# Graph counting stage: tile steps spread over twelve pairs, projection evicted by ScalarE

## The chip, the cores and the metric

The kernel runs on one core of one Trainium2 chip. The metric is the device time of the whole program in microseconds (us). A core has five engines that run side by side and meet only at semaphores: TensorE (PE in the profile, PEld its weight loads) multiplies into eight PSUM banks, VectorE (DVE) and ScalarE (ACT) do elementwise work, GpSimd (POOL) and SyncE (SP) mostly move data here.

## The reference, cut to what matters

Two graph layers, each followed by a mixture-of-experts layer, on 1250 nodes with 512 features and 40000 edges. What the change touches is the first layer:

```python
for h in range(8):                                   # heads
    Wx = x @ Ws[h] + Wb[h]                           # x: layer-normed rows, [1250, 64] per head
    s = Wx[v_tgt] @ a_w[h, :d] + Wx[v_src] @ a_w[h, d:] + a_b[h]
    alpha = segment_softmax(leaky_relu(s), v_tgt)    # over the edges of a target
    outs.append(segment_sum(alpha * Wx[v_src], v_tgt))
```

The kernel never gathers by edge. It first counts how many edges run from each source to each target, a dense matrix of counts, and does the softmax and the sums with matmuls on that matrix.

## The kernel before, in words

The nodes are ten tiles of 128. The **counting stage** works off 184 *pairs* (a group of 384 sorted edges with a window of 16 targets), in 23 batches of eight. For a pair VectorE writes one-hot matrices of the edges' sources and targets (`onehot`), TensorE multiplies them, three matmuls of 160 columns (`count`), and adds what the window already holds with an identity matmul (`merge`), and ScalarE writes the sum back (`write_batch`). A batch's one-hots are written in two halves of four pairs. A half waits for `counted` at a pair about two batches back, since the one-hots have two buffers; `merge(k)` waits until ScalarE has written pair k-2. Each batch TensorE and ScalarE load eight window addresses into registers at its sixth pair (`targets`).

Everything else of the first layer's front half is threaded between the pairs. For a tile t: VectorE takes the row statistics (`ln_stats`), ScalarE a square root (`ln_sqrt`), VectorE the reciprocal (`ln_scale`), ScalarE writes the normed rows (`ln_norm`), TensorE transposes them into bank 6 (`tile_T`), ScalarE copies the upper fp16 part (`ln_copy`), VectorE makes the lower part (`xT_low`), and TensorE then does twelve products of 512 columns with the projection weights, each with one of 16 columns for the attention scores (`lin_a`, j from 0 to 11). Last, the two sums are scaled and get their bias (`evac_a`, on VectorE). In the kernel before one tile is begun per batch: `BEGIN` puts tile t at batch 1+t, its transposes at the third pair of batch 2+t, its products in batch 3+t by `LIN_SLOTS`, its eviction into the middle of batch 5+t. So ten batches carry tiles, and the last ones hold only the second layer's weight transposes (`second_weights`, four steps, from batch 12), the score thresholds, and the exponentials with two loads of ScalarE's function table (batches 19 and 20).

Each engine runs its own list in the order written. After the last pair is written (`hist_done`) all engines turn to the per-head matmuls.

Of the kernel before, what the change touches and what calls it, by code (L numbers as in the profile page):

```python
# [8 lines left out]
F16 = mybir.dt.float16  # L9
# [5 lines left out]
P = 128  # L15
# [15 lines left out]
LB = 8  # L31
# [24 lines left out]

BEGIN = {1 + t: t for t in range(T)}
LIN_SLOTS = ((0,), (1, 2), (), (3, 4), (5, 6), (7,), (8, 9), (10, 11))
B_GW = max(BEGIN) + 2
B_CS = B_GW + K  # L60
B_EXP = B_CS + 3
AHEAD = 3
# [4 lines left out]
def gnn_ffn_kernel(nc, x_d, src_d, dst_d, Ws_d, Wb_d, aw_d, ab_d, Wg_d, bg_d, We_d, be_d, gW_d, gb_d,  # L67
                   Wr_d, br_d, W1_d, b1_d, W2_d, b2_d, out_d):
    ctx = ExitStack()
    with ctx:  # L70
# [92 lines left out]
        hi16, o = carve(num_words, o, [GE], F16)  # L163
        src_i = be_bc[:, 0:GE].bitcast(I32)
        VP, o = carve(big, 0, [T, 2, H, 2, FE], F16)
        nacc, o = carve(big, o, [T, H, FE])
# [249 lines left out]
        def _(g):  # L416
# [15 lines left out]
            nc.gpsimd.iota(iota_lo, [[1, P]], base=0, **kw)  # L432
            nc.gpsimd.memset(ones16, 1.0)
            nc.gpsimd.iota(iota_q, [[1, RW]], base=1, **kw).then_inc(sem("consts"), 1)
            nc.gpsimd.memset(zero[:, 0, :], 0.0).then_inc(sem("zero_set"), 1)
# [77 lines left out]
        def _(a):  # L513
# [26 lines left out]
            def exponential(i):  # L540
# [7 lines left out]
                if i == 3:  # L548
                    act(A2, e2t, ACT.Exp).then_inc(sem("exps"), 1)

            def write_batch(base, at, middle):

                for k in range(LB):
                    if not isinstance(base, int):
                        a.wait_ge(sem("counted"), base + (k + 1))
                    ins = act(counts_at(at[k], k), count_bank(base, k)[:, 0:RW].rearrange("p (d s) -> p s d", s=T), ACT.Copy)  # L556
                    if isinstance(base, int):
                        ins.wait_op(sem("counted"), base + (k + 1), "sem-ge")
                    ins.then_inc(sem("written"), 1)
                    middle(k)  # L560
# [37 lines left out]
            for b in range(NB):  # L598
                if b in BEGIN:
                    ln_sqrt(BEGIN[b])  # L600

                def middle(k):
                    if k == 1 and b - 1 in BEGIN:
                        t = BEGIN[b - 1]
# [7 lines left out]
                    if k == 3 and b - 1 in BEGIN:  # L612
                        t = BEGIN[b - 1]
# [8 lines left out]
                if b == 1:  # L622
                    a.wait_ge(sem("wa_psum"), 1)
                    act(Wa[:, 0, :, :].rearrange("p k c -> p (k c)"), bank[5][:, 0:K * 2 * H], ACT.Copy, scale=WS)
                    act(cb, bank[5][:, K * 2 * H:(K + 1) * 2 * H], ACT.Copy).then_inc(sem("weight_hi"), 1)
                if b - B_GW in range(K):
# [207 lines left out]
        def _(v):  # L834
# [146 lines left out]
            def value(h):  # L981

                if h:
                    v.wait_ge(sem("v_lo"), h)
                V.tensor_tensor(vtmp, Wx[:, :, h, :].unsqueeze(1).to_broadcast([P, 2, T, FE]),  # L985
                                bc(B12[:, :, :, h], [P, 2, T, FE]), ALU.mult).then_inc(sem("v_made"), 1)

            pair_tables(0)
            for b in range(NB):
                if b == 1:  # L990
                    v.wait_ge(sem("ld_x"), 64)
                if b in BEGIN:
                    ln_stats(BEGIN[b], x[:, BEGIN[b], :])
                if b - 2 - B_GW in range(K):
# [4 lines left out]
                if b == NB - 1:  # L999
                    last_onehots(b)  # L1000
                elif b:
                    half_onehots(b, 0)
                    if b - 4 in BEGIN:
                        evac_a(BEGIN[b - 4])
                        if BEGIN[b - 4] == T - 1:
                            scores()
                    half_onehots(b, 1)
# [9 lines left out]
                if b == 3:  # L1017
                    v.wait_ge(sem("weight_hi"), 2)
                    V.scalar_tensor_tensor(Wa[:, 1, :, :].rearrange("p k c -> p (k c)"), bank[5][:, 0:K * 2 * H], WS,
                                           Wa[:, 0, :, :].rearrange("p k c -> p (k c)"), ALU.mult, ALU.subtract).then_inc(sem("weight_lo"), 1)  # L1020
                if b - 1 in BEGIN:
                    ln_scale(BEGIN[b - 1])
                if b - 2 in BEGIN:
                    t = BEGIN[b - 2]
                    xT_low(t, bank[6], xTs[:, t % 2, :, :, :])
            v.wait_ge(sem("exps"), 4)
# [330 lines left out]
        def _(pe):  # L1357
# [39 lines left out]
            def lin_a(t, j):  # L1397
                k, i = divmod(j, len(PASSES))
                xp, wp = PASSES[i]
                if j == 0:  # L1400
                    if t == 0:
                        pe.wait_ge(sem("weight_lo"), 2)
                    pe.wait_ge(sem("xT_ready"), t + 1)
                    if t >= 2:
                        pe.wait_ge(sem("evacA"), t - 1)
                xt = xTs[:, t % 2, xp, k, :]
                last = j == K * len(PASSES) - 1
                mm(bank[2 + t % 2][:, :], xt, W016[:, wp, k, :], start=j == 0, stop=last)  # L1408
                ins = mm(bank[4 + t % 2][:, 0:2 * H], xt, Wa[:, wp, k, :], start=j == 0, stop=last)
                if last:  # L1410
# [15 lines left out]
            def thresholds():  # L1426
                pe.wait_ge(sem("thr_made"), 1)
                pe.wait_ge(sem("weight_lo"), 2 + K)
                for i, n in enumerate((4, 4, 2)):
# [52 lines left out]
            def between(b, k):  # L1482
                if b - 2 in BEGIN:
                    for j in LIN_SLOTS[k]:
                        lin_a(BEGIN[b - 2], j)
                if k == 2 and b - 1 in BEGIN:
                    t = BEGIN[b - 1]
# [344 lines left out]
```

## Time and profile before

| | us |
|---|---|
| median of 3 runs | 567.69 (564.15, 567.69, 568.19) |
| the profiled execution's own time | 565.49 |
| its span in the trace | 563.7 |
| counting stage: first count to the write of the last pair | 21.4 to 146.8 |
| busy: TensorE, VectorE, ScalarE over the span | 88%, 84%, 61% |

In the rows of a timeline the first number is the start in us from the span's start, the second how long the row's instructions took together; "[0.43 <-PE ...]" is idle time before it and what ended it. Instructions of one engine overlap a little, so what one adds to its engine is read from start to start. TensorE's busy time shows matmuls in flight, and is no measure of how much more fits in.

### The profile page before, as it was taken

Reading aid. Unit: us, or ns where it says so; the run is one execution under the profiler, and the core shown is the slowest. Engines: PE = TensorE matmul, PEld = TensorE weight load, DVE = VectorE, ACT = ScalarE, POOL = GpSimd, SP = SyncE. Lnnn points to the kernel's source line nnn. Section 1 sums busy time; section 2 is a strip of 40 time slices with the busy share of each in tenths; the row PEclk is TensorE's granted clock in tenths of the full one; section 3 lists DMA queues with packets and bytes.
Section 4 is the critical chain, followed back from the end, with each engine's and each line's share of the span. In section 5 each row is a group of like instructions: output and inputs, shape, how many; then the busy total and the mean of one; then the engine's idle time right before and its main releaser. Section 6 shows DMA issues by size and latency. Waiting matters only on the chain.

```text
span 563.7 us, 12125 instructions
## 1 busy us (share of the span) xinstructions
PE 498.4 (88%) x4635; PEld 369.9 (66%) x4636; DVE 473.0 (84%) x933; ACT 342.4 (61%) x663; POOL 68.7 (12%) x83
## 2 busy tenths in 40 slices
PE   1869999877589999999889899988899999889995
PEld 1757777666488888889767644444466696557662
DVE  7999999799899999995899758995877787768771
ACT  5365555567889999995575533344545457756820
POOL 3000000000000000000000020223244420212242
PEclk9999999999899999999999989999999999999998
DMA  6980000002001111100000068000001119776111
GB/s 175 351 290 2 1 2 1 2 6 93 3 27 66 53 48 49 49 3 1 1 1 2 0 215 325 1 1 1 4 20 59 57 55 354 262 234 222 60 53 52
DMA packets 25306, 45.14 MB, mean 80 GB/s; under 512 B 6961, under 2 KB 7205, under 8 KB 25248
## 3 DMA queue, kind: packets, MB, share of 16 engines
q1 hardware_dynamic: 23264, 39.16, 20.4%
q0 software_dynamic: 1952, 5.18, 2.5%
q8 instruction: 39, 0.64, 0.5%
q14 instruction: 19, 0.16, 0.1%
q10 hardware_dynamic: 32, 0.01, 0.0%
HBM read 33.23 MB, written 11.95 MB: 80 GB/s over the span
## 4 chain that ended last, share of the span: by engine, by line
PE 52%; DVE 33%; issue 8%; ACT 3%; DMA 2%; POOL 1%; ACTq 0%; SPq 0%; POOLq 0%; DVEq 0%
PE bank L1384 7%; PE bank L1774 7%; PE bank L1650 5%; PE bank L1408 5%; PE bank L1451 4%; DVE work L1080 4%; DVE big L948 4%; PE bank L1745 4%; PE bank L1458 4%; PE bank L1555 3%; PE bank L1362 3%; PE bank L1568 2%; DVE rings L1080 2%; DVE st L847 2%; DVE work L985 1%
## 5 line engine op out<-in xcount | busy, mean ns | idle before, releaser
L948 DVE TENSOR_TENSOR big<-mid 128x1536 f16<-128x1536 f16 (+1 forms) x100 | 92.0, 979 | 0.0
L1555 PE MATMUL bank<-big,work 128*128 128x130 f16 x1080 | 67.3, 224 | 8.4 <-DVE work L1080 8.4
L1451 PE MATMUL bank<-big 128*128 128x160 f16 x552 | 70.9, 245 | 4.1 <-DVE big L948 4.1
L1555 PEld LDWEIGHTS bank<-big,work 128*128 128x128 f16 x1080 | 64.1, 100 | 10.4 <-DVE work L1080 4.9
L1451 PEld LDWEIGHTS bank<-big 128*128 128x128 f16 x552 | 50.9, 110 | 6.7 <-DVE big L948 6.3
L657 ACT ACTIVATE mid<-aux,small 128x1280 f16<-128x1280 f32 x36 | 47.4, 1349 | 0.7 <-DVE work L1080 0.4
L1568 PE MATMUL bank<-big,mid 128*128 128x260 f16 x400 | 47.1, 275 | 0.1
L1650 PE MATMUL bank<-mid 128*128 128x512 f16 x200 | 47.2, 378 | 0.0
L556 ACT ACTIVATE big<-bank 128x160 f32 x92 | 27.9, 303 | 26.7 <-PE bank L1458 25.3
L556 ACT ACTIVATE mid<-bank 128x160 f32 x92 | 27.7, 302 | 25.5 <-PE bank L1458 22.5
L1568 PEld LDWEIGHTS bank<-big,mid 128*128 128x128 f16 x400 | 38.2, 96 | 7.5 <-issue 0.3
L518 ACT ACTIVATE sd<-ve 128x1 f32<-128x1 f32 x40 | 8.0, 200 | 51.6 <-DVE ve L849 51.6
L1408 PE MATMUL bank<-big,rings 128*128 128x512 f16 x120 | 38.6, 378 | 0.0
L1458 PE MATMUL bank<-mid,ident 128*128 x92 | 27.7, 302 | 9.1 <-ACT mid L556 4.8
L847 DVE BATCH_NORM_STATS2 st<-row 128x6 f32<-128x512 f32 x40 | 27.6, 691 | 8.5 <-POOL row L489 7.8
L1555 PE MATMUL bank<-big,rings 128*128 128x130 f16 x520 | 32.0, 220 | 2.6 <-DVE rings L1080 1.6
L531 ACT ACTIVATE rings<-row,nm,rs 128x512 f32<-128x512 f32 x30 | 24.3, 810 | 13.5 <-DVE nm L865 13.5
L1555 PEld LDWEIGHTS bank<-big,rings 128*128 128x128 f16 x520 | 29.9, 98 | 3.7 <-DVE rings L1080 2.2
L1650 PEld LDWEIGHTS bank<-mid 128*128 128x128 f16 x200 | 19.7, 104 | 18.0
L473 POOL DMA_INDIRECT out<-aux x16 | 22.2, 1388 | 76.6 <-DVE aux L1303 74.2
L457 POOL TENSOR_TENSOR mid<-mid,ident 128x128 f16<-128x128 f16 x10 | 3.9, 424 | 215.9 <-DVE small L1134 215.9
L523 ACT ACTIVATE rings<-bank 128x512 f16<-128x512 f32 (+1 forms) x30 | 17.8, 593 | 18.3 <-PE bank L1362 18.3
(313 smaller groups left out, 1122.9 us busy)
## 6 DMA issues: line engine op xcount, KB each, us to landing
big<-in_L_ffn_W SPq DMA_DIRECT2D x10, 1024.0 KB, 8.8
mid<-in_L_ffn_W SPq DMA_DIRECT2D x6, 1024.0 KB, 14.4
xperm_scratch<-work SPq DMA_DIRECT2D x1, 5753.0 KB, 19.4
aux<-thr_scratch SPq DMA_DIRECT2D x8, 640.0 KB, 3.8
aux<-xperm_scratch SPq DMA_DIRECT2D x8, 523.0 KB, 3.8
row<-in_x SPq DMA_DIRECT2D x1, 2304.0 KB
aux<-in_L_gnn_Ws SPq DMA_DIRECT2D x4, 256.0 KB, 4.5
work<-in_L_gnn_W SPq DMA_DIRECT2D x1, 1024.0 KB, 14.6
```

The costliest lines, as they stand in the source:

```text
L556: ins = act(counts_at(at[k], k), count_bank(base, k)[:, 0:RW].rearrange("p (d s) -> p s d", s=T), ACT.Copy)
L657: act(zmask[i % NZ], thr_bc[:, h % 2, :], ACT.Sigmoid, bias=steep[:, s, h:h + 1], scale=-STEEP).then_inc(sem("z_made"), 1)
L847: link(V.bn_stats(st[:, i, :], xt))
L948: return V.tensor_tensor(out.rearrange("p c (v two) -> p c v two", two=2), values.rearrange("p (v two) -> p v two", two=2).unsqueeze(1).to ...
L1384: ins = mm(out, xt16[:, xp, k, :], w16[:, wp, k, :], start=i == 0 and k == 0, stop=i == 2 and k == K - 1)
L1408: mm(bank[2 + t % 2][:, :], xt, W016[:, wp, k, :], start=j == 0, stop=last)
L1451: mm(count_bank(base, k)[:, 0:RW], L_ring[:, slot, k * CH + j, :], R_ring[:, slot, k * CH + j, :], start=j == 0, stop=False)
L1458: ins = mm(count_bank(base, k)[:, 0:RW].rearrange("p (d s) -> p s d", s=T), ident16[:, :], counts_at(at[k], k), start=False, stop=True)
L1555: ins = mm(acc_region(h, t), weighted[i % NC][:, t * P:(t + 1) * P], VP[:, s, part, h, :, :].rearrange("p b f -> p (b f)"), start=False, s ...
L1568: ins = mm(bank[2 * (t % 2) + g2][:, 0:4 * FE].rearrange("p (h f) -> p h f", f=FE), C[:, s, t * P:(t + 1) * P], VP[:, s, part, 4 * g2:4 * ...
L1650: ins = mm(bank[6 + t % 2][:, :], C[:, s, t * P:(t + 1) * P], hp[:, s, part, :], start=s == 0 and part == 0, stop=s == T - 1 and part == 1)
L1774: ins = mm(bank[4 + 2 * (e % 2) + j][0:m, :], hT16[:, e % 2, hp_, k, j * P:j * P + m], W16[e % 2][1][:, wp, k, :], start=False, stop=n == ...
```

## The change

The schedule of a tile is no longer bound to batches. Tables give each step its place: VectorE's by half batches (`STATS_H`, `SCALE_H`, `LOW_H`, every three halves), ScalarE's and TensorE's by pairs (`SQRT_P`, `NORM_P`, `ROWS_P`, `COPY_P`, `LIN_P`, `EVAC_P`, every twelve pairs). The ten tiles so take pairs 24 to 143 instead of 24 to 103. The eviction is ScalarE's, a plain scaled copy; the bias is added by TensorE as one more product ahead of the twelve (its two fp16 parts stand in 64 partitions of `Wb16` and `cb16`). VectorE makes the lower parts of these once, at batch 2. The second layer's weight steps begin at batch 17 instead of 12, `scores` moves to batch 19, the exponentials to batch 21, the second table load to batch 22.

```diff
-BEGIN = {1 + t: t for t in range(T)}
-LIN_SLOTS = ((0,), (1, 2), (), (3, 4), (5, 6), (7,), (8, 9), (10, 11))
-B_GW = max(BEGIN) + 2
+HALF = LB // 2
+STEP = 3 * HALF
+STATS_H = {2 + 3 * t: t for t in range(T)}
...
+LOW_H = {6 + 3 * t: t for t in range(T)}
+SQRT_P = {7 + STEP * t: t for t in range(T)}
+NORM_P = {15 + STEP * t: t for t in range(T)}
+ROWS_P = {17 + STEP * t: t for t in range(T)}
+COPY_P = {18 + STEP * t: t for t in range(T)}
+LIN_SLOTS = ((0,), (1,), (2,), (3,), (4,), (), (5,), (6,), (7,), (8, 9), (10,), (11,))
+LIN_P = {24 + STEP * t + i: (t, js) for t in range(T) for i, js in enumerate(LIN_SLOTS)}
+EVAC_P = {24 + STEP * (t + 1): t for t in range(T)}
+SCORES_H = max(EVAC_P) // HALF + 2
+B_GW = max(ROWS_P) // LB + 2
...
+            def evac_a(t):
+
+                a.wait_ge(sem("linA"), t + 1)
+                act(Wx[:, t, :, 0:F], bank[2 + t % 2][:, :].rearrange("p (h f) -> p h f", h=H), ACT.Copy, scale=1.0 / WS)
+                act(sc[:, t, :], bank[4 + t % 2][:, 0:2 * H], ACT.Copy, scale=1.0 / WS).then_inc(sem("evacA"), 1)
...
-                act(cb, bank[5][:, K * 2 * H:(K + 1) * 2 * H], ACT.Copy).then_inc(sem("weight_hi"), 1)
+                act(cb16[0:64, :], bank[5][0:64, K * 2 * H:(K + 1) * 2 * H], ACT.Copy, scale=WS)
+                a.wait_ge(sem("ld_x"), 64)
+                act(Wb16[0:64, :], Wb_bc[0:64, :, :].rearrange("p h f -> p (h f)"), ACT.Copy, scale=WS).then_inc(sem("weight_hi"), 1)
...
-            def evac_a(t):
-                v.wait_ge(sem("linA"), t + 1)
-                V.scalar_tensor_tensor(Wx[:, t, :, 0:F], bank[2 + t % 2][:, :].rearrange("p (h f) -> p h f", h=H), 1.0 / WS, Wb_bc,
-                                       ALU.mult, ALU.add)
-                V.scalar_tensor_tensor(sc[:, t, :], bank[4 + t % 2][:, 0:2 * H], 1.0 / WS, cb, ALU.mult, ALU.add).then_inc(sem("evacA"), 1)
...
+            def tile_step(u):
+                if u in STATS_H:
+                    ln_stats(STATS_H[u], x[:, STATS_H[u], :])
+                if u in SCALE_H:
+                    ln_scale(SCALE_H[u])
+                if u in LOW_H:
+                    t = LOW_H[u]
+                    xT_low(t, bank[6], xTs[:, t % 2, :, :, :])
+                if u == SCORES_H:
+                    scores()
...
+                    for half in range(2):
+                        tile_step(2 * b + half)
+                        half_onehots(b, half)
...
+                    mm(bank[2 + t % 2][:, :], part32[0:64, 0:1].to_broadcast([64, P]), Wb16[0:64, :], start=True, stop=False)
+                    mm(bank[4 + t % 2][:, 0:2 * H], part32[0:64, 0:1].to_broadcast([64, P]), cb16[0:64, :], start=True, stop=False)
```

How the lists of the engines change is seen at three places. First VectorE, one tile's round of the kernel before (1536 and 1920 columns are the one-hots of a half batch, four pairs):

```order
L864 RECIPROCAL rs<-sd 128x1
L865 SCALAR_TENSOR_TENSOR nm<-mv,rs 128x1
L870 TENSOR_TENSOR rings<-bank6,rings 128x512
L847 BN_STATS st<-row 128x6
L848 BN_AGGR mv<-st 128x2
L849 TENSOR_SCALAR ve<-mv 128x1
L948 TENSOR_TENSOR big<-mid 128x1536
L948 TENSOR_TENSOR big<-mid 128x1920
L890 SCALAR_TENSOR_TENSOR mid<-bank2,aux 128x8x64
L892 SCALAR_TENSOR_TENSOR small<-bank4,small 128x16
L948 TENSOR_TENSOR big<-mid 128x1536
L948 TENSOR_TENSOR big<-mid 128x1920
```

and the round that takes its place, from the lower part of one tile (`bank6`, line 895) on:

```order
L895 TENSOR_TENSOR rings<-bank6,rings 128x512
L967 TENSOR_TENSOR big<-mid 128x1536
L967 TENSOR_TENSOR big<-mid 128x1920
L889 RECIPROCAL rs<-sd 128x1
L890 SCALAR_TENSOR_TENSOR nm<-mv,rs 128x1
L967 TENSOR_TENSOR big<-mid 128x1536
L967 TENSOR_TENSOR big<-mid 128x1920
L872 BN_STATS st<-row 128x6
L873 BN_AGGR mv<-st 128x2
L874 TENSOR_SCALAR ve<-mv 128x1
L967 TENSOR_TENSOR big<-mid 128x1536
L967 TENSOR_TENSOR big<-mid 128x1920
```

A tile's round holds three halves instead of two and no eviction, and the lower part of tile t stands directly ahead of the one-hots of pairs 24+12t to 27+12t, where it stood ahead of those of batch 4+t.

Second ScalarE in the changed kernel, from the copy of the upper part (line 538, pair 18+12t) to the eviction of the tile before (lines 569 and 570, pair 24+12t):

```order
L538 ACTIVATE rings<-bank6 128x512
L577 ISA
L577 ACTIVATE big<-bank1 128x10x16
L533 ACTIVATE sd<-ve 128x1
...
L577 ACTIVATE mid<-bank0 128x10x16
L569 ACTIVATE mid<-bank2 128x8x64
L570 ACTIVATE small<-bank4 128x16
L577 ISA
L577 ACTIVATE big<-bank1 128x10x16
```

Between the copy and the first count of pair 24+12t lie six pairs; in the kernel before there were thirteen between the copy and the one-hots that stand behind the lower part.

Third TensorE in the changed kernel, the start of a tile's products at pair 24+12t (lines 1428 and 1429 are the bias) and the transposes of the next at pair 29+12t (line 1384):

```order
L1481 MATMUL bank<-mid,ident 128x10x16
L1474 MATMUL bank<-big 128x160 x3
L1428 MATMUL bank<-be_bc 128x512
L1429 MATMUL bank<-be_bc 128x16
L1432 MATMUL bank<-big,rings 128x512
L1433 MATMUL bank<-small,rings 128x16
...
L1481 MATMUL bank<-big,ident 128x10x16
L1474 MATMUL bank<-big 128x160 x3
L309 TENSOR_LOAD mid
L1384 MATMUL bank<-ident,rings 128x128 x4
```

The products come mostly one to a pair instead of one or two, the bias is new, and for every second tile the address load (line 309) stands right before the transposes.

## Rows read from the trace of the kernel before

**Rows 1.** Busy us of PE, PEld, DVE, ACT, POOL in a stretch; clock; DMA.

```profile
40.00:50.00 10.00, 9.74 (x96) 7.35 (x94) 9.83 (x20) 6.07 (x20) 0.00 (x0) 1.00 0.01 3
```

**Rows 2.** Timeline of VectorE over one batch with a tile.

```profile
60.16 2.02 DVE L948 TENSOR_TENSOR big<-mid 128x1536 f16<-128x1536 f16 x2
62.09 0.68 DVE L890 SCALAR_TENSOR_TENSOR mid<-bank,aux 128x512 f32<-128x512 f32 x1
...
62.78 2.02 DVE L948 TENSOR_TENSOR big<-mid 128x1536 f16<-128x1536 f16 x2
64.71 0.15 DVE L864 RECIPROCAL rs<-sd 128x1 f32<-128x1 f32 x1
...
64.98 0.68 DVE L870 TENSOR_TENSOR rings<-bank,rings 128x512 f16<-128x512 f32 x1
65.58 0.68 DVE L847 BATCH_NORM_STATS2 st<-row 128x6 f32<-128x512 f32 x1
...
66.58 2.02 DVE L948 TENSOR_TENSOR big<-mid 128x1536 f16<-128x1536 f16 x2
```

**Rows 3.** Timeline of TensorE in the same batch: merges (L1458) and transposes (L1362).

```profile
61.03 0.30 PE L1458 MATMUL bank<-mid,ident 128*128 x1
...
61.64 0.63 PE L1362 MATMUL bank<-ident,rings 128*128 128x128 f32 x4
62.10 0.30 PE L1458 MATMUL bank<-big,ident 128*128 x1
...
65.99 0.30 PE L1458 MATMUL bank<-mid,ident 128*128 x1
...
66.58 0.30 PE L1458 MATMUL bank<-big,ident 128*128 x1
```

**Rows 4.** Timeline of ScalarE there: the normed rows and the upper part.

```profile
60.73 0.80 ACT L531 ACTIVATE rings<-row,nm,rs 128x512 f32<-128x512 f32 x1
...
62.64 0.59 ACT L523 ACTIVATE rings<-bank 128x512 f16<-128x512 f32 x1
```

**Rows 5.** Timelines of ScalarE, VectorE and TensorE: two handovers that were waited for.

```profile
94.51 0.59 ACT L523 ACTIVATE rings<-bank 128x512 f16<-128x512 f32 x1
...
95.13 0.69 DVE L870 TENSOR_TENSOR rings<-bank,rings 128x512 f16<-128x512 f32 x1 [0.23 <-ACT rings L523]
...
111.75 3.09 DVE L948 TENSOR_TENSOR big<-mid 128x1920 f16<-128x1920 f16 x3
...
114.90 0.38 PE L1451 MATMUL bank<-big 128*128 128x160 f16 x3 [0.37 <-DVE big L948]
```

**Rows 6.** Timelines of ScalarE, VectorE and TensorE before the first tile's products.

```profile
30.08 0.30 ACT L556 ACTIVATE big<-bank 128x160 f32 x1
...
32.21 2.29 DVE L1015 SCALAR_TENSOR_TENSOR big<-aux,big 128x2048 f16<-128x2048 f32 x1 [0.68 <-ACT big L621]
...
40.36 0.31 PE L1458 MATMUL bank<-mid,ident 128*128 x1
```

**Rows 7.** Timelines of VectorE, TensorE and ScalarE behind the last tile.

```profile
104.31 0.69 DVE L997 SCALAR_TENSOR_TENSOR mid<-bank,mid 128x512 f16<-128x512 f32 x1 [3.56 <-ACT mid L629]
...
105.37 0.31 PE L1458 MATMUL bank<-mid,ident 128*128 x1
...
105.73 0.30 PE L1458 MATMUL bank<-big,ident 128*128 x1
...
106.59 0.31 PE L1458 MATMUL bank<-mid,ident 128*128 x1 [0.35 <-ACT big L556]
...
122.59 1.31 ACT L633 ACTIVATE work<-bank 8x512 f32<-8x512 f32 x3
...
131.22 0.30 ACT L556 ACTIVATE mid<-bank 128x160 f32 x1 [0.17 <-PE bank L1458]
...
144.40 1.50 DVE L985 TENSOR_TENSOR work<-mid,small 128x1300 f32<-128x1300 f32 x1
...
146.47 0.30 ACT L556 ACTIVATE big<-bank 128x160 f32 x1
```

More of the change, by code:

```diff
@@ L54 @@
 RW32 = 6
-BEGIN = {1 + t: t for t in range(T)}
-LIN_SLOTS = ((0,), (1, 2), (), (3, 4), (5, 6), (7,), (8, 9), (10, 11))
-B_GW = max(BEGIN) + 2
-B_CS = B_GW + K
-B_EXP = B_CS + 3
+HALF = LB // 2
+STEP = 3 * HALF
+STATS_H = {2 + 3 * t: t for t in range(T)}
+SCALE_H = {4 + 3 * t: t for t in range(T)}
+LOW_H = {6 + 3 * t: t for t in range(T)}
[8 more added lines that the diff above has]
+B_GW = max(ROWS_P) // LB + 2
+B_CS = SCORES_H // 2
+B_EXP = B_CS + 2
 AHEAD = 3
@@ L164, in gnn_ffn_kernel @@
         src_i = be_bc[:, 0:GE].bitcast(I32)
+        Wb16, o = carve(be_bc, 0, [D], F16)
+        cb16, o = carve(be_bc, o, [2 * H], F16)
+        part32, _ = carve(be_bc, 400, [2], F16)
         VP, o = carve(big, 0, [T, 2, H, 2, FE], F16)
@@ L433, in _ @@
             nc.gpsimd.memset(ones16, 1.0)
+            nc.gpsimd.memset(part32, 1.0 / 32)
             nc.gpsimd.iota(iota_q, [[1, RW]], base=1, **kw).then_inc(sem("consts"), 1)
@@ L598, in _ @@
             for b in range(NB):
-                if b in BEGIN:
-                    ln_sqrt(BEGIN[b])
                 def middle(k):
-                    if k == 1 and b - 1 in BEGIN:
-                        t = BEGIN[b - 1]
+                    i = b * LB + k
+                    if i in SQRT_P:
+                        ln_sqrt(SQRT_P[i])
+                    if i in EVAC_P:
+                        evac_a(EVAC_P[i])
+                    if i in NORM_P:
+                        t = NORM_P[i]
                         ln_norm(t, x[:, t, :], xh_ring[:, t % 2, :])
@@ L611, in middle @@
                         act(sd[0:1, 0:1], zero16[0:1, 0:1], ACT.Sigmoid)
-                    if k == 3 and b - 1 in BEGIN:
-                        t = BEGIN[b - 1]
+                    if i in COPY_P:
+                        t = COPY_P[i]
                         if t >= 2:
@@ L991, in _ @@
                     v.wait_ge(sem("ld_x"), 64)
-                if b in BEGIN:
-                    ln_stats(BEGIN[b], x[:, BEGIN[b], :])
                 if b - 2 - B_GW in range(K):
@@ L1001, in _ @@
                 elif b:
[L1002 to L1007, printed above, removed]
+                    for half in range(2):
+                        tile_step(2 * b + half)
+                        half_onehots(b, half)
                 else:
@@ L1016, in _ @@
                                            ALU.mult, ALU.subtract).then_inc(sem("weight_lo"), 1)
-                if b == 3:
                     v.wait_ge(sem("weight_hi"), 2)
                     V.scalar_tensor_tensor(Wa[:, 1, :, :].rearrange("p k c -> p (k c)"), bank[5][:, 0:K * 2 * H], WS,
[L1020 to L1025, printed above, removed]
+                                           Wa[:, 0, :, :].rearrange("p k c -> p (k c)"), ALU.mult, ALU.subtract)
+                    V.scalar_tensor_tensor(cb16[32:64, :], bank[5][32:64, K * 2 * H:(K + 1) * 2 * H], WS, cb16[32:64, :], ALU.mult, ALU.subtract)
+                    V.scalar_tensor_tensor(Wb16[32:64, :], Wb_bc[32:64, :, :].rearrange("p h f -> p (h f)"), WS, Wb16[32:64, :],
+                                           ALU.mult, ALU.subtract).then_inc(sem("weight_lo"), 1)
             v.wait_ge(sem("exps"), 4)
@@ L1405, in lin_a @@
                         pe.wait_ge(sem("evacA"), t - 1)
+                    mm(bank[2 + t % 2][:, :], part32[0:64, 0:1].to_broadcast([64, P]), Wb16[0:64, :], start=True, stop=False)
+                    mm(bank[4 + t % 2][:, 0:2 * H], part32[0:64, 0:1].to_broadcast([64, P]), cb16[0:64, :], start=True, stop=False)
                 xt = xTs[:, t % 2, xp, k, :]
                 last = j == K * len(PASSES) - 1
-                mm(bank[2 + t % 2][:, :], xt, W016[:, wp, k, :], start=j == 0, stop=last)
-                ins = mm(bank[4 + t % 2][:, 0:2 * H], xt, Wa[:, wp, k, :], start=j == 0, stop=last)
+                mm(bank[2 + t % 2][:, :], xt, W016[:, wp, k, :], start=False, stop=last)
+                ins = mm(bank[4 + t % 2][:, 0:2 * H], xt, Wa[:, wp, k, :], start=False, stop=last)
                 if last:
@@ L1427, in thresholds @@
                 pe.wait_ge(sem("thr_made"), 1)
-                pe.wait_ge(sem("weight_lo"), 2 + K)
                 for i, n in enumerate((4, 4, 2)):
@@ L1482, in between @@
             def between(b, k):
[L1483 to L1487, printed above, removed]
+                i = b * LB + k
+                if i in LIN_P:
+                    t, js = LIN_P[i]
+                    for j in js:
+                        lin_a(t, j)
+                if i in ROWS_P:
+                    t = ROWS_P[i]
                     if t >= 1:
```

## The prediction, made before the changed kernel ran

> **What bounds the kernel now.** I read the span in slices, then the counting stage alone, since nothing behind it is edited and all engines meet at its end. With tiles in it, VectorE and TensorE both look full: 9.83 and 9.74 of 10 us, ScalarE 6.07 [rows 1]. So the waits and the start-to-start times must decide.
>
> VectorE's batch with a tile: two halves of one-hots at 1.93 (60.16 to 62.09), eviction 0.69, scale 0.27, lower part 0.60, statistics 1.00 [rows 2]; in all 6.42. TensorE's: I read it by *slots*, from merge to merge. An empty slot is 0.35 (105.37 to 105.73), one with a product pair 0.59, so a product is 0.24; the slot with transposes is 1.07, of which 0.46 lies behind their start [rows 3, 7]. Eight slots, twelve products and one set of transposes are 2.8 + 2.9 + 0.7 = 6.4. The two engines are level by chance, and neither waits. The transposes start at 61.64 only because the normed rows end at 61.53 [rows 4].
>
> Behind the last tile VectorE is first the bound, but not at the end: it finishes its one-hots at 144.40, while the last write starts at 146.47. From 131.22 there are 31 slots in 15.25 us: 10.9 of slots, three address loads at 0.51 (0.86 less 0.35, the slot from 105.73), and 2.9 for the two table loads with their exponentials [rows 7]. The stage's end belongs to the chain of TensorE and ScalarE.
>
> **The parts.**
>
> *Start, up to pair 24.* The first square root moves from behind ScalarE's copy of the weights to the write of pair 7, which ends at 30.38, but VectorE now wants its result before the one-hots of pair 16. So VectorE: scale until 30.85, a half to 32.8, statistics and a half to 35.7, the weights' lower part (2.21, from 32.21 to the next instruction in [rows 6]; the fp16 upper part is ready) to 37.9. Then three small products, two of them new: I take 0.85 for all, 0.6 of it for the 512 columns of the bias as for the lower part. Then lower part 0.60 and one-hots 2.02: pair 24 can be counted at 41.5 or 41.6. Before, its count came right behind the merge at 40.36 [rows 6]. Cost: **1.1**.
>
> *Eviction.* VectorE loses 10 x 0.69 = 6.9. ScalarE gets it, about 0.6 for 512 columns as its copy [rows 4] and 0.1 to 0.2 for 16. It has two slots of slack there, and 3.9 of 10 us idle [rows 1]; nothing in the tile stage. *Bias.* One product per tile, 0.24, on TensorE: 2.4.
>
> *Spreading.* A tile's round is now twelve pairs. VectorE: 3 x 1.93 + 1.87 = 7.66. TensorE: 12 x 0.35 + 13 x 0.24 + transposes. The normed rows are asked for a slot later than before (written at pair 15, used at 17), so I take the transposes without their wait, 0.46: 7.8. Between 7.8 and 8.05 with it.
>
> *The handover.* This is where I see the loss. From the start A of the transposes: ScalarE's copy starts at A+1.00 (61.64 to 62.64), ends at A+1.59 [rows 3, 4]; VectorE takes it 0.03 later (95.10 to 95.13) [rows 5]; lower part 0.60, one half of one-hots until 2.02 later; TensorE's count starts 0.06 after that (114.84 to 114.90) [rows 2, 5]. Sum: the count of pair 24+12t can start at A+4.30. TensorE wants it after 0.46, five slots with six products (0.59 x 4 + 0.83) and 0.09 more: A+3.74. The change has put the lower part directly ahead of the very one-hots that TensorE needs next, so it waits 0.56 a tile, and its products behind the count wait too. From the count to the next A: 4.06. The round is 4.30 + 4.06 = **8.36**, and VectorE with 7.66 idles in it. Nothing removed from VectorE shortens this loop.
>
> The first A after pair 24 is 45.4 (41.8 for its merge, a slot of 0.83, four of 0.59, 0.37), the tenth tile's is eight rounds on, 112.3. From it to the merge of pair 144: 4.2, then thirteen slots with twelve products, and one set of weight transposes, 8.4: **124.9**.
>
> *Behind pair 144.* All second-layer steps now stand there. 39 slots 13.7; four address loads 2.1; three weight steps with transposes and copies 2.3; the thresholds' ten transposes (by the four, 1.1) and their copies 1.3 [rows 7], together 2.4; ScalarE's last eviction, which delays its next write, 0.5; the table loads 2.7 to 2.9; two waits for one-hots, since `scores` now stands in front of them, 0.8. Sum **24.5**; VectorE needs four batches, 15.4, and 4 for the rest, so it is not the bound. Last write at 149.4 against 146.47: **+2.9**.
>
> The start and the loop have no row of their own yet. Bounds: without any wait in the handover the rounds are 7.8, five us less over nine tiles, and the total is -2.1. With the transposes' wait back in all nine (0.25 each) and an address load in front of every second set not hidden (five at 0.51) it is +7.7. I take the middle value, as its durations are rows of the same instructions in the same sequence.
>
> In the stretch of [rows 1] TensorE's weight loads are busy 74%, VectorE 98%, ScalarE 61%. The Trainium skill, "Perfetto Trace Analysis", section "Identifying the Most-Contended Engine", says to take the engine with the highest occupancy and optimize it first, judging TensorE by its weight loads instead of its matmuls. By that rule VectorE would be the one to relieve; it is the first rival. The slots above, which have no gap that a faster VectorE could fill, speak against it.
>
> **The sum.** The profiled execution took 565.49, so 568.4 in its terms. The median of the runs is 2.2 higher, 567.69, which gives 570.6. The three runs spread over 4 us; I say **570**. About 1%, 5.7 us, is what a measurement of this kernel tells from no change.
>
> **Rivals.**
> 1. *VectorE sets the pace throughout.* It loses 6.9, gains 0.7 for the bias parts, and its wait of 3.56 for the weights [rows 7] goes: 6 to 10 less, 558 to 562. For it: 98% busy, no waits from 40 to 95. Against: TensorE has none either, and the end of the stage is not VectorE's. 0.15.
> 2. *The handover costs nothing*, as ScalarE copies sooner or VectorE's half is quicker than its rows: TensorE's rounds of 7.8, -2.1, so 565.5. Against: each link is a measured one. 0.2.
> 3. *The loop is longer than counted, slower by over 1%.* Mechanism: transposes, copy, lower part, one-hots, count stand in one closed chain, so anything more in it is paid nine times: the transposes' own wait (0.25), the address load that stands before them (0.51 for five of them). It passes 1% from 0.3 us a round on; at its full price +7.7, about 575.5. Against: with products queued, the load at the sixth pair costs nothing in the batch of [rows 2, 3]. 0.2.
>
> **How the numbers follow.** The forecast has 0.45. Faster by over 1%: most of rival 1, with a little for what I don't see, 0.13. Slower by over 1%: rival 3 and the forecast's upper edge, 0.24. Within 1%: 0.63. The range 561 to 576 holds forecast, rivals 2 and 3 and rival 1's weak end.
>
> **What would show it.** Right: rounds between two sets of transposes of tiles 2 to 9 at 8.3 to 8.5; TensorE waiting 0.5 for VectorE's one-hots once a round; VectorE idle 0.6 or 0.7 a round, released by ScalarE's copy; pair 144 near 125 and the last write near 149.5. Rounds of 7.8 with no wait: rival 2. Rounds of 7.66 with VectorE never idle: rival 1. Rounds of 8.7 and more: rival 3. Wrong in another way: if the stretch behind pair 144 is far from 24.5, or if TensorE's granted clock, 1.00 here, falls in the small waits.

## The result and the profile after

The changed kernel takes 571.02 us (median of 18 runs, 568.17 to 575.36) against 567.86 for the kernel before (18 runs, 564.15 to 573.77): ratio 1.0066, 95% interval 1.0044 to 1.0088. It is slower by 3.2 us, within 1%, and the forecast of 570 with +2.9 stands. Its profiled execution took 574.16, with a span of 572.4 and a mean granted clock of 0.976 (565.49, 563.7 and 0.988 before).

**The handover**, in the timelines of TensorE, ScalarE and VectorE of the changed kernel (start, us, engine, line; in brackets the idle time before the row and what ended it):

```profile
48.80 0.63 PE L1384 MATMUL bank<-ident,rings 128*128 128x128 f32 x4
...
49.80 0.59 ACT L538 ACTIVATE rings<-bank 128x512 f16<-128x512 f32 x1
...
50.42 0.69 DVE L895 TENSOR_TENSOR rings<-bank,rings 128x512 f16<-128x512 f32 x1 [0.51 <-ACT rings L538]
51.03 2.02 DVE L967 TENSOR_TENSOR big<-mid 128x1536 f16<-128x1536 f16 x2
...
53.11 0.38 PE L1474 MATMUL bank<-big 128*128 128x160 f16 x3 [0.38 <-DVE big L967]
...
57.26 0.60 PE L1384 MATMUL bank<-ident,rings 128*128 128x128 f32 x4
```

Read it as a ring. The transposes start at 48.80, the copy 1.00 later, VectorE's lower part 0.03 after the copy's end, its one-hots 0.61 later, and TensorE's count of pair 36 at 53.11: 4.31 after the start, where the sum from [rows 2 to 5] gave 4.30. The next transposes come 4.15 behind that count. The last transposes start at 116.68, eight rounds behind those of 48.80: 8.49 each. The waits of the stretch say the same:

```profile
DVE rings L895 <- ACT rings L538: 7.6, 10, 1.8
...
PE bank L1474 <- DVE big L967: 4.1, 10, 0.9
```

(Total us, times, longest.) VectorE waits for ScalarE's copy in all ten tiles, TensorE for VectorE's one-hots in all ten. In the tile stage of the kernel before there was one wait of the first kind, 0.23 [rows 5], and none of the second; VectorE has time left and TensorE cannot use it.

**The slot with the bias** is the second thing, in TensorE's timeline:

```profile
53.57 0.30 PE L1481 MATMUL bank<-mid,ident 128*128 x1
...
54.00 0.39 PE L1428 MATMUL bank<-be_bc 64*128 64x512 f16 x1
...
54.59 0.30 PE L1481 MATMUL bank<-big,ident 128*128 x1
```

From merge to merge this slot takes 1.02; with two ordinary products it would be 0.83, as by [rows 3, 7] an empty slot is 0.35 and a product 0.24. The bias costs 0.43, not 0.24.

**The start.** The clock of TensorE fell there, which it had not in the profile before. Windows of five us (us, busy us of PE, PEld, DVE, ACT, POOL, granted clock, DMA share, GB/s) and two rows of the timelines:

```profile
20.00:25.00 5.00, 3.33 (x36) 3.13 (x34) 4.83 (x12) 1.70 (x5) 0.00 (x0) 1.00 1.09 343
25.00:30.00 5.00, 5.00 (x34) 4.96 (x33) 1.64 (x2) 0.84 (x3) 0.00 (x0) 0.60 1.05 376
30.00:35.00 5.00, 3.85 (x22) 3.07 (x22) 1.76 (x4) 2.72 (x6) 0.00 (x0) 0.50 1.06 376
35.00:40.00 5.00, 4.78 (x31) 4.49 (x32) 4.93 (x7) 2.84 (x10) 0.00 (x0) 0.54 0.84 300
```

```profile
32.78 0.30 ACT L577 ACTIVATE big<-bank 128x160 f32 x1
32.97 0.20 ACT L533 ACTIVATE sd<-ve 128x1 f32<-128x1 f32 x1
...
33.20 0.16 DVE L889 RECIPROCAL rs<-sd 128x1 f32<-128x1 f32 x1 [6.56 <-ACT sd L533]
...
44.83 0.38 PE L1474 MATMUL bank<-big 128*128 128x160 f16 x3 [0.94 <-DVE big L967]
```

At 0.50, which is 1.2 GHz, an empty slot of TensorE takes 0.67 instead of 0.35. ScalarE's write of pair 7 starts at 32.78, where it was 30.08 in the kernel before [rows 6]; the moved square root stands behind it, and VectorE idles 6.56 us in front of the reciprocal. Pair 24 is counted at 44.83; 41.5 was forecast.

**The end of the stage**, in the timelines of TensorE and ScalarE:

```profile
129.37 0.30 PE L1481 MATMUL bank<-mid,ident 128*128 x1
...
145.30 1.28 ACT L558 ACT_TABLE_LOAD   x1
...
147.11 0.31 PE L1481 MATMUL bank<-big,ident 128*128 x1 [1.26 <-ACT big L577]
...
153.62 0.30 ACT L577 ACTIVATE big<-bank 128x160 f32 x1
```

Pair 144 is merged at 129.37, the last write starts at 153.62: 24.25 for the stretch, 24.5 forecast. From that write to the end of the span are 418.8 us, 417.2 before. That part takes 416.5 to 419.6 us in the fourteen profiles of this document, though no edit touches it, so single profiles are not compared by their whole span.

### The profile page after: what moved, and what is told of

Read it like the earlier page. It is cut to its first block, busy times and chain, and to the rows that moved or that the text cites. A ratio compares the mean times of both kernels' runs of the same rounds, so it can differ in the third digit from the quotient of the medians.

```text
span 572.4 us, 12168 instructions
## 1 busy us (share of the span) xinstructions
PE 508.2 (89%) x4655; PEld 377.0 (66%) x4656; DVE 467.7 (82%) x915; ACT 347.2 (61%) x684; POOL 69.0 (12%) x84
## 4 chain that ended last, share of the span: by engine, by line
PE 51%; DVE 33%; issue 8%; ACT 5%; DMA 1%; POOL 1%; ACTq 1%; POOLq 0%; DVEq 0%
PE bank L1406 7%; PE bank L1799 7%; PE bank L1675 5%; PE bank L1474 4%; DVE work L1102 4%; DVE big L967 4%; PE bank L1770 4%; PE bank L1481 3%; PE bank L1384 3%; PE bank L1580 3%; PE bank L1432 3%; PE bank L1593 2%; DVE rings L1102 2%; DVE st L872 1%; DVE work L1004 1%
## 5 line engine op out<-in xcount | busy, mean ns | idle before, releaser
L1474 PE MATMUL bank<-big 128*128 128x160 f16 x552 | 76.9, 254 | 5.8 <-DVE big L967 4.1
L1474 PEld LDWEIGHTS bank<-big 128*128 128x128 f16 x552 | 54.6, 114 | 9.3 <-DVE big L967 8.7
L1432 PE MATMUL bank<-big,rings 128*128 128x512 f16 x120 | 44.2, 380 | 0.0
L1481 PE MATMUL bank<-big,ident 128*128 x92 | 28.4, 309 | 1.7 <-ACT big L577 1.7
```

The costliest lines, as they stand in the source:

```text
L1432: mm(bank[2 + t % 2][:, :], xt, W016[:, wp, k, :], start=False, stop=last)
L1474: mm(count_bank(base, k)[:, 0:RW], L_ring[:, slot, k * CH + j, :], R_ring[:, slot, k * CH + j, :], start=j == 0, stop=False)
L1481: ins = mm(count_bank(base, k)[:, 0:RW].rearrange("p (d s) -> p s d", s=T), ident16[:, :], counts_at(at[k], k), start=False, stop=True)
```

## The experiments

All runs are compared in three stretches of the counting stage, cut at ScalarE's writes, which the trace holds completely. Starts of the writes in us from the span's start, times as medians, ratios to the kernel before with 95% intervals. "Clock" is the granted clock of TensorE from 20 to 40 us, the mean of four windows of 5 us. "Late scale" is the kernel two pairs earlier with the first scale moved (3); the three rows below it start from that kernel. The time is the median of 10 runs, but of 18 for the changed kernel, 8 with the early load, 6 with both, and only 4 one pair later and with the eviction alone. Each ratio is against runs of the kernel before made alongside; the changed kernel itself read 571.02 and 574.13 on two occasions, so a difference of times between two rows tells little below 3 us, and the stretches tell more.

```
kernel          clock   write of 24  24 to 144  144 to 183  last write  time     ratio
before           1.00     40.71       86.64      19.12       146.47
before, again    0.69     43.12       86.56      19.12       148.80
changed          0.66     45.38       84.42      23.82       153.62    571.02   1.0066 [1.0044, 1.0088]
changed, again   0.66     45.41       84.41      23.82       153.64    574.13   1.0093 [1.0048, 1.0138]
one earlier      0.92     43.13       83.43      23.83       150.39    570.97   1.0049 [1.0024, 1.0074]
one later        0.58     45.89       92.26      23.63       161.78    581.45   1.0251 [1.0185, 1.0316]
evict on DVE     0.74     44.76       84.52      24.28       153.56    572.39   1.0098 [1.0065, 1.0130]
eviction alone   0.92     41.79       90.10      19.27       151.16    572.31   1.0121 [1.0065, 1.0177]
spread alone     0.74     44.34       82.46      24.28       151.08    569.86   1.0055 [1.0023, 1.0086]
two earlier      0.74     44.95       80.38      23.64       148.97    567.82   0.9988 [0.9953, 1.0022]
 + late scale    1.00     41.76       79.38      23.83       144.97    565.05   0.9965 [0.9931, 0.9999]
 + wide bias     0.58     44.51       77.60      23.64       145.75    563.93   0.9945 [0.9910, 0.9981]
 + early load    0.66     44.39       79.36      22.45       146.20    563.89   0.9911 [0.9863, 0.9959]
 + both          0.92     40.89       77.62      22.44       140.95    562.00   0.9897 [0.9854, 0.9940]
```

**1. The kernels themselves again.** The changed one, unedited:

> The changed kernel itself, once more, as the yardstick of this set. In its first profile TensorE ran at the lower granted clock (0.50 to 0.60) from 25 to 39 us, and the count of pair 24 came at 44.8 instead of the 41.5 that was forecast. Theory 1 (that dip is a matter of the single run): here it is missing or elsewhere, pair 24 is counted at 41 to 42, and rounds from transposes to transposes are 8.5 again. Theory 2 (the change itself brings the dip on, since VectorE waits for the early square root): it is there again at the same place. Time 1.005 to 1.009 of before.

The three stretches came within 0.03 us of the first profile. The clock fell at the same place.

And the kernel before, once more, for its clock:

> The kernel before, for one more profile. Question: does its TensorE also fall to the lower granted clock in the start-up between 20 and 40 us, and what does it cost there? Theory (the dip is common to both kernels): the granted clock of runs of the kernel before, 0.971 to 0.991, spreads like that of the changed one, so a profile with a mean below 0.98 shows the dip, and the last write comes 2 us or so later than 146.5. Rival (only the changed schedule has it): the start is at full clock whatever the mean.

```profile
25.00:30.00 5.00, 4.46 (x38) 3.83 (x36) 4.93 (x8) 1.38 (x6) 0.00 (x0) 0.75 1.05 373
30.00:35.00 5.00, 4.24 (x24) 3.48 (x23) 4.63 (x6) 3.52 (x9) 0.00 (x0) 0.50 1.06 376
35.00:40.00 5.00, 4.13 (x24) 3.66 (x24) 4.59 (x10) 2.38 (x9) 0.00 (x0) 0.50 0.76 271
```

The fall does not need the change: here the kernel before has it as well, nearly in the same windows. It costs that kernel 2.41 us up to pair 24 and nothing in the rest of the counting stage. Whether the change makes it likelier is open: twelve of the fourteen profiles have it between 20 and 45 us, for 3.4 to 17.1 us, and of the kernel before there are only two, one with and one without. With the fall on both sides the last write of the changed kernel is 4.8 later: +2.3 up to pair 24, -2.1 in the tiles, +4.7 behind pair 144.

**2. The handover, one pair earlier and one later.** If the ring is the bound, moving its first link moves every round; if VectorE's or TensorE's sum of work is, nothing moves.

```diff
-NORM_P = {15 + STEP * t: t for t in range(T)}
-ROWS_P = {17 + STEP * t: t for t in range(T)}
-COPY_P = {18 + STEP * t: t for t in range(T)}
+NORM_P = {14 + STEP * t: t for t in range(T)}
+ROWS_P = {16 + STEP * t: t for t in range(T)}
+COPY_P = {17 + STEP * t: t for t in range(T)}
```

> One table edit: norm, transposes and copy of every tile one pair earlier (14, 16, 17 instead of 15, 17, 18). Handover theory: the count of pair 24+12t is wanted 0.59 later after the transposes, 4.33 against the 4.31 that the handover takes; TensorE's wait for the one-hots vanishes, rounds fall from 8.49 to 7.9, the kernel by 9 x 0.6 = 5 us to 0.996 or 0.997 of before. Rival (TensorE's own work sets the rounds, the wait is only where its slack shows): nothing changes, 1.006.

The later one has 16, 18 and 19:

> The same three steps one pair later (16, 18, 19). Handover theory: the loop gets a slot longer, rounds 9.1, nine rounds and more make 5 us, 1.015 of before. Rival (slack of TensorE): the wait just grows smaller elsewhere, 1.006.

Later by one, the rounds grew to 9.14 to 9.36, 9.19 in the mean, and the time rose to 1.0251 of the kernel before [1.0185, 1.0316]. That is 7.3 us more than the changed kernel alongside, where 5 had been expected. In its profile the stretch with the tiles is 7.8 longer: eight rounds at 0.7, and the way from the first set of transposes to the second, 10.57 for 8.70. TensorE's timeline there shows it in one round:

```profile
51.48 0.63 PE L1384 MATMUL bank<-ident,rings 128*128 128x128 f32 x4
55.88 0.38 PE L1474 MATMUL bank<-big 128*128 128x160 f16 x3 [1.05 <-DVE big L967]
60.62 0.63 PE L1384 MATMUL bank<-ident,rings 128*128 128x128 f32 x4
```

Earlier by one, the rounds did not all fall: they alternate between 8.53 to 8.59 and 8.13. ScalarE's and TensorE's timelines of such a round:

```profile
46.15 0.64 PE L1384 MATMUL bank<-ident,rings 128*128 128x128 f32 x4
...
46.96 0.30 ACT L577 ACTIVATE big<-bank 128x160 f32 x1 [0.76 <-PE bank L1481]
47.55 0.60 ACT L538 ACTIVATE rings<-bank 128x512 f16<-128x512 f32 x1 [0.29 <-issue]
...
50.87 0.38 PE L1474 MATMUL bank<-big 128*128 128x160 f16 x3 [0.16 <-DVE big L967]
```

In every second tile the copy stands at the sixth pair of a batch, where ScalarE loads its eight addresses first. It starts 1.40 behind the transposes (47.55 less 46.15) instead of 1.00, and the wait stays. In the tiles between, whose copy meets no load, it is 1.01 (54.68 to 55.69). That link was in none of my sums. The short rounds of 8.13 are still 0.2 over those of the next experiment; what that is stays open.

**3. Two pairs earlier** (13, 15 and 16), past that load:

> Norm, transposes and copy of every tile two pairs earlier than in the changed kernel (13, 15, 16). With one pair earlier every second round was down to 8.13 without a wait, the others at 8.55, where ScalarE's address load at the sixth pair of a batch stood just ahead of the copy. Handover theory: two pairs earlier the copy never meets that load, all rounds are 8.13, TensorE never waits; about 2 us below one pair earlier, 1.001 or 1.002 of before. Rival (the rounds of 8.55 come from TensorE's own address load): the same alternation stays, 1.005.

TensorE has no wait left between 48 and 112 us, and the rounds are flat, 0.2 under the 8.13 that had been expected:

```profile
48.47 0.63 PE L1384 MATMUL bank<-ident,rings 128*128 128x128 f32 x4
...
56.39 0.63 PE L1384 MATMUL bank<-ident,rings 128*128 128x128 f32 x4
```

7.92 each, the 7.8 forecast for TensorE's own slots and 0.12 more, and the loss is gone: 0.9988 [0.9953, 1.0022]. The two pairs take 4.0 us out of the stretch with the tiles (80.38 for 84.42), which is more than the change lost. With the first scale half a batch later as well,

```diff
-SCALE_H = {4 + 3 * t: t for t in range(T)}
+SCALE_H = {4 + 3 * t + (t == 0): t for t in range(T)}
```

> As early2, and the scale of tile 0 alone half a batch later, so that VectorE writes one more half of one-hots before it waits for the first square root. VectorE's start is then bound by ScalarE's bias copies at 37.5: pair 24 is counted 0.4 earlier in a run without a clock dip, more (1 to 2 us) with one, in which VectorE waited 6.6 us there. 1.000 of before, 0.5 to 1 us below early2. Rival (the start is TensorE's and ScalarE's, and VectorE's wait there is hidden): the same as early2.

the time is 565.05, which the ratios alone don't set apart from the one above. Its profile had no fall of the clock, so its start (41.76) can't be held against the 44.95 of the one above; two later kernels with this edit and an even lower clock wrote pair 24 at 44.39 and 44.51, 0.4 to 0.6 earlier. The moved scale is worth that at least.

**4. The parts of the change apart.** First the changed kernel with its eviction back on VectorE, as two scaled copies, the bias product kept:

```diff
+EVAC_H = {11 + 3 * t: t for t in range(T)}
...
+            def evac_v(t):
+                v.wait_ge(sem("linA"), t + 1)
+                V.tensor_scalar(Wx[:, t, :, 0:F], bank[2 + t % 2][:, :].rearrange("p (h f) -> p h f", h=H), 1.0 / WS, None, ALU.mult)
...
+                if u in EVAC_H:
+                    evac_v(EVAC_H[u])
```

> The eviction goes back to VectorE (two scaled copies at the half batch 11+3t), all else as in the changed kernel, the bias still TensorE's. Handover theory: VectorE has 0.7 to 0.8 idle in each round and the eviction takes 0.7, so rounds stay at 8.5 and the time within 1 us of the changed kernel (1.006 of before). Rival (VectorE's load is the bound after all): rounds 9.2, 6 to 7 us more, 1.018.

The tile stretch is 84.52, 0.1 more than with the eviction on ScalarE. In its waits the row of VectorE for the copy has shrunk from 7.6 to

```profile
DVE rings L888 <- ACT rings L539: 1.8, 3, 1.1
```

so the evictions filled the holes in front of the lower parts. VectorE's own round grew from 7.66 to 8.35, and the rounds stayed at 8.46 to 8.65. Taking 6.9 us off VectorE was worth nothing in this order of steps: this refutes rival 1 directly.

Then the tables without the bias product, eviction with bias on VectorE at the same place:

> The other half of the change alone: the tile steps by the tables over twelve pairs as in the changed kernel, but the eviction with its bias on VectorE (half batch 11+3t) and no bias product. Handover theory: the loop loses the 0.43 of the bias, 8.06; VectorE's round is 7.66 + 0.69 = 8.35 and so the bound; rounds 8.3 to 8.4, 1 us or so below the changed kernel, 1.004 to 1.006 of before. Rival (spreading is a gain, and the bias product eats it): 0.998 or less.

82.46 in the tiles, 1.96 less than the changed kernel, or 0.2 a tile. The product's 0.43 is gone from TensorE, but VectorE now has 8.35 of its own in a round (7.66 and the 0.69 of the eviction) and has become the later one; the rounds are 8.33 in the mean: TensorE waits ten times for one-hots, 6.4 us in all. VectorE's timeline:

```profile
57.35 0.68 DVE L886 TENSOR_TENSOR rings<-bank,rings 128x512 f16<-128x512 f32 x1
```

The lower part here follows the half before it without waiting for the copy. This also bounds the reading above: with the eviction on VectorE rounds can hardly be shorter than its 8.35, so the rounds of 7.92 and 7.73 in 3 and 5 should need it on ScalarE. That is an estimate from these rows; no run has the earlier handover with the eviction on VectorE. And last the kernel before, tables untouched, with ScalarE's eviction (first pair of batch 4+t) and the bias product:

> The kernel before with one half of the change alone: the eviction is ScalarE's (behind the first pair of batch 4+t) and the bias a product of TensorE, all other steps at their old places. TensorE theory: a batch with a tile takes 6.38 + 0.43 (what the bias costs in the changed kernel) = 6.8 us on TensorE, 4.3 more over ten, VectorE's release gives back at most the one eviction behind them; 3 to 4 us slower, 1.005 to 1.007. Rival (VectorE was the bound of the tile batches, with 98% busy): a batch falls from 6.42 towards 6.38 or less and the wait behind them goes, 0.985 to 0.995.

The batch with a tile grew from 6.38 to 6.81, from one set of transposes to the next:

```profile
57.57 0.63 PE L1372 MATMUL bank<-ident,rings 128*128 128x128 f32 x4
...
61.92 0.30 PE L1470 MATMUL bank<-mid,ident 128*128 x1
62.94 0.30 PE L1470 MATMUL bank<-big,ident 128*128 x1
...
64.38 0.63 PE L1372 MATMUL bank<-ident,rings 128*128 128x128 f32 x4
```

That is the 0.43 of the bias (its slot, with one product beside it, is again 1.02), paid in each tile: ten are 4.3, and the stretch from pair 24 to 144 grew by 3.5. TensorE has no wait between two tiles' transposes here, while VectorE idles 0.9 to 2.2 a tile from the fourth one on, for the copy. The time is 1.0121 [1.0065, 1.0177] over four runs, more than I had put on record (1.005 to 1.007) and more than its profile's 570.47 shows.

**5. The price of the bias product.** It runs over 64 partitions among products over 128. The same product over all 128, weights 1/64 for 1/32, on top of the last kernel of 3:

```diff
-            nc.gpsimd.memset(part32, 1.0 / 32)
+            nc.gpsimd.memset(part32, 1.0 / 64)
...
-                    mm(bank[2 + t % 2][:, :], part32[0:64, 0:1].to_broadcast([64, P]), Wb16[0:64, :], start=True, stop=False)
-                    mm(bank[4 + t % 2][:, 0:2 * H], part32[0:64, 0:1].to_broadcast([64, P]), cb16[0:64, :], start=True, stop=False)
+                    mm(bank[2 + t % 2][:, :], part32[:, 0:1].to_broadcast([P, P]), Wb16, start=True, stop=False)
+                    mm(bank[4 + t % 2][:, 0:2 * H], part32[:, 0:1].to_broadcast([P, P]), cb16, start=True, stop=False)
```

> early2_start with the bias product over 128 partitions instead of 64 (weights 1/64, upper parts in 64 of them, lower in the others). A slot with the bias took 1.02 where the columns alone would make 0.83. Theory (the extra 0.19 comes from switching to a product of 64 rows and back): it vanishes, rounds fall from 7.92 to 7.75, 2 us less, 0.993. Rival (the extra belongs to the two products themselves, their short second one or their broadcast weights): 7.92 stays, as early2_start.

TensorE's timeline of the kernel with 64 partitions:

```profile
49.40 0.30 PE L1481 MATMUL bank<-mid,ident 128*128 x1
49.49 0.41 PE L1474 MATMUL bank<-big 128*128 128x160 f16 x3
49.83 0.39 PE L1428 MATMUL bank<-be_bc 64*128 64x512 f16 x1
50.06 0.17 PE L1429 MATMUL bank<-be_bc 64*128 64x16 f16 x1
50.16 0.39 PE L1432 MATMUL bank<-big,rings 128*128 128x512 f16 x1
...
50.42 0.30 PE L1481 MATMUL bank<-big,ident 128*128 x1
```

and with 128:

```profile
52.14 0.30 PE L1481 MATMUL bank<-mid,ident 128*128 x1
52.23 0.41 PE L1474 MATMUL bank<-big 128*128 128x160 f16 x3
52.48 0.38 PE L1428 MATMUL bank<-be_bc 128*128 128x512 f16 x1
52.70 0.17 PE L1429 MATMUL bank<-be_bc 128*128 128x16 f16 x1
52.73 0.38 PE L1432 MATMUL bank<-big,rings 128*128 128x512 f16 x1
...
52.97 0.30 PE L1481 MATMUL bank<-big,ident 128*128 x1
```

The slot falls from 1.02 to 0.83. Start to start, 0.09 goes ahead of the first product of 64 rows (0.34 to 0.25) and 0.07 behind the second (0.10 to 0.03), the rest in steps of 0.01 and 0.02 beside them. The rounds fall to 7.73. The Trainium skill, "TensorEngine Tiling (Array Packing)", section "Key Properties", says that a change of tiling mode, unlike a change of tile, drains TensorE. The rows agree: the gaps stand where the kernel goes from 128 rows to 64 and back, and go when it doesn't. That what fills them is a drain, no row shows. The page gives no price; it is 0.19 us for the two changes here.

**6. The table load.** ScalarE's first load stands at pair 168, where TensorE waits for each write. A tiny exponential at pair 140 brings it forward:

```diff
+                    if i == 140:
+                        act(sd[0:1, 0:1], zero16[0:1, 0:1], ACT.Exp)
```

> early2_start with a tiny exponential at pair 140, where ScalarE has slack between products, so that the table for the exponentials is loaded there and not at pair 168, where TensorE waited 1.26 for it. Theory (the stage behind pair 144 is the chain of TensorE and ScalarE, and each stall in it counts in full): 1.0 to 1.2 us less, 0.994. Rival (VectorE's four batches bound that stretch): no change.

The load in ScalarE's timeline, now among the tile's products:

```profile
120.61 0.30 ACT L577 ACTIVATE mid<-bank 128x160 f32 x1 [0.28 <-PE bank L1483]
120.93 1.28 ACT L627 ACT_TABLE_LOAD   x1
122.23 0.20 ACT L627 ACTIVATE sd<-zero 1x1 f32<-1x1 f16 x1
122.34 0.28 ACT L577 ACTIVATE big<-bank 128x160 f32 x1
```

TensorE has no wait from 118 to 124 us, and the tile stretch is unchanged (79.36 against 79.38). The last stretch is 22.45 against 23.83: the wait of 1.26 at the first load is gone, and the load costs nothing where TensorE has products to fill the time. In the ratios, 0.9911 for 0.9965, the gain is not clear of the noise; the stretches show it. The second load still costs its 1.18.

**7. All together.**

> The last three gains together: normed rows, transposes and copy two pairs earlier with the first scale half a batch later, the bias product over all 128 partitions (weights of 1/64), and ScalarE's first table load moved to pair 140. Theory (the handover loop, TensorE's slots and the table load are separate terms that add): rounds 7.73 as with the wide bias product alone, a stretch of 22.4 from the write of pair 144 to that of pair 183 as with the early table load alone, so the last write comes at 144.97 - 1.7 - 1.4 = 141.9 if the granted clock does not fall between 20 and 40 us, and near 144.4 if it does; the time is about 3 us under that of the first of the three (565.1), so 562, ratio 0.988 to 0.991. Rival (they hide one another, as the removed waits fall on the same slots): ratio 0.993 or more, last write 143 or later without the fall of the clock.

562.0 us, 0.9897 of the kernel before [0.9854, 0.9940], about 9 us under the changed kernel as it was. The stretches add to within 0.02 us: 77.62 as with the wide bias, 22.44 as with the early load. The start came 0.9 earlier than I had assumed for a profile without the fall of the clock, though the clock fell here too, from 31.5 us on for 3.4 us; by then the write of pair 7 (29.26) was through.

## Why the prediction was right

*What bounds it.* TensorE's chain, not VectorE's 98%. Shown: with 6.9 us of evictions put back on VectorE the rounds stay at 8.5, and with the eviction moved in the kernel before the rounds grow by exactly the product put on TensorE. The two engines stay close: 8.35 of VectorE's own a round is enough to bind it in the tables without the bias product.

*Eviction, worth nothing.* Right for this order of steps, by the same two runs. By the rule of the Trainium skill weighed in the prediction ("Perfetto Trace Analysis", "Identifying the Most-Contended Engine") VectorE was the one to relieve; the runs speak against it here. Even in the changed kernel, where VectorE idles 0.5 to 0.8 a round for the copy, it is the busiest by that count (9.10, against 6.76 of weight loads and 5.86 of ScalarE):

```profile
60.00:70.00 10.00, 9.39 (x89) 6.76 (x87) 9.10 (x15) 5.86 (x20) 0.00 (x0) 1.00 0.00 0
```

*Bias, 0.24 a tile.* Too small: 0.43, since the change from 128 rows to 64 and back costs 0.19 more. This is a price that no row of before held.

*TensorE's round without waits, 7.8.* Measured 7.92 with the narrow product and 7.73 with the wide one; 7.8 stands but for the 0.19.

*The handover.* The mechanism was right and link by link of the right size: 4.31 for 4.30. The round is 8.49 for 8.36. The difference lies in the leg from the count to the next transposes, 4.15 and 4.26 in turn where I had 4.06, and that leg holds the bias product with its 0.19. Nine times 0.13 are 1.2 us. From the last transposes to the merge of pair 144 it is 12.69 for 12.6 (the 8.4 in that sum needs a thirteenth product, the bias; with the twelve it names it would be 8.15). The sign "TensorE waiting 0.5" came smaller, 0.34 to 0.38 of idle time, but opening the ring took 0.57 off a round (8.49 to 7.92), which is the 0.56 of the forecast.

*Rival 2* (rounds of 7.8, no wait) describes the kernel with the tables two pairs earlier, not this one. *Rival 3* did not come: with the address load ahead of the transposes the leg up to them is 4.26 instead of 4.15, so it costs 0.1 in every second round and not the 0.51 that was weighed. But a relative of it is real, the address load on ScalarE's queue ahead of the copy, and it is what spoils the version that is one pair earlier.

*Behind pair 144.* 24.25 for 24.5; of its terms only the table loads have been read singly, 1.26 and 1.18 for 2.7 to 2.9 with their exponentials. Against the kernel before this stretch is the dearest part, +4.7 from the write of pair 144 on, since second-layer steps that stood ahead of that pair now stand behind it. No run put them back to batch 12 with the new tables, so what their place costs is not shown.

*The start.* Mis-sized by 3.3 (44.83 for 41.5). The forecast had VectorE take up its scale behind ScalarE's write of pair 7, and put that write where it was in the profile before. It came 2.7 later (32.78 for 30.08), and VectorE's scale is done at 33.48 where 30.85 was forecast: 2.6. From there to the count of pair 24 are 11.35 us for 10.65: 0.38 of waiting for ScalarE's copy, 0.19 more for the weights' lower part (2.40 for 2.21) and 0.15 more for the three small products (1.00 for 0.85). The wait of 6.56 us in front of the reciprocal is not the clock's alone. In the profile of one pair earlier the clock was 1.00 up to 32 us, and VectorE still idled 4.24 us there, as the new order of steps has it:

```profile
30.88 0.16 DVE L889 RECIPROCAL rs<-sd 128x1 f32<-128x1 f32 x1 [4.24 <-ACT sd L533]
```

The kernel before lost 2.4 up to pair 24 with the fall of its clock. What made the clock fall stays open: the same program shows 1.00 from 20 to 40 us in one execution, and 0.50 for 13.7 us in another.

*The sum.* In the profile the last write is 4.2 later than forecast (153.62 for 149.4): 3.3 of start, 1.2 of rounds, 0.25 less behind. Against the kernel before with the same fall of the clock it is 4.8 later, where +2.9 was forecast, with start and rounds about 1.2 short each. The medians differ by 3.2, and their interval, 2.5 to 5.0 us, holds both numbers; on the second occasion the ratio was 1.0093, some 5 us. So the direction and the ring are no luck, but that the total of 571.02 lies only 1.0 above the forecast is in part: two of its terms were too small.

## What to carry to other kernels

When work moves off a full engine, follow the ring of handovers instead of the shares: find the consumer that wants the result first, add up the links from the producer to it, and compare that with what the consumer has queued in between. A step in a round-robin table needs slack for everything on its queue, address loads included; two pairs more of it here turned a loss into a tie. An engine relieved for nothing in one order of steps can be the bound in the next: look at the shares again once the ring is open. And put a table load or another long stall where the other engine has work queued, not where it waits for every result.

## What the runs showed of the hardware that I had not expected

- A product over 64 partitions among products over 128 takes as long itself (0.38 to 0.39 for 512 columns) but adds 0.19 us of gaps around it.
- An address load of eight values on ScalarE delayed the copy behind it by 0.40 us.
- A table load of 1.28 us cost TensorE 1.26 and 1.18 where it waited for each write, and nothing among the products.
- TensorE's clock can be granted at 0.50 for 3 to 17 us between 23 and 41 us while DMA moves some 370 GB/s, in one execution of a program and not in another. TensorE had been busy 3.3 us of the window from 20 to 25 us ahead of the fall in the changed kernel, 3.9 ahead of it in the kernel before, and 3.6 in the kernel before without a fall, so this count does not tell the cases apart. It cost the kernel before 2.4 us.
